# A decoder layer in float32 on one core: the opening staged by halves of columns, row maxima by quadrants, context products last, and indirect stores in a queue of their own

## What is computed

```python
def layernorm(x): return (x - mean(x)) / sqrt(var(x) + 1e-5)
# 1. self-attention, 16 heads of 16, ALiBi slopes 0.5**h
q, k, v = split(heads(layernorm(x) @ qkv_w.T + qkv_b))
scores = q @ k.T / 4 - abs(i - j) * slope[h]
x = x + (softmax(scores) @ v) @ out_w.T + out_b
# 2. cross-attention on 77 context rows, one head of 256
y = layernorm(x); a = softmax((y @ Wq.T + bq) @ (ctx @ Wk.T + bk).T / 16) @ (ctx @ Wv.T + bv)
x = x + (y + a) @ Wo.T + bo
# 3. mixture of 8 experts (256 -> 1024 -> 256), top 2 by the router
y = layernorm(x); w = softmax over the two largest of y @ W_router + b_router
x = x + sum over the two: w[e] * (relu(y @ W1[e] + b1[e]) @ W2[e] + b2[e])
```

## Time and profile before

| | |
|---|---|
| runs | 1726.36, 1726.41, 1731.1 us; median 1726.41 |
| the profiled execution | 1725.03 us, of which the span is 1723.2 |
| busy | PE 94%, DVE 59%, ACT 46%, POOL 19% of the span |
| mean granted PE clock | 0.976 of full |

### The profile page before, as it was taken

The page is one execution under the profiler, slowest core; times in us unless marked ns, Lnnn a source line. Parts: engine busy times, 40 slices in busy tenths (PEclk is TensorE's granted clock), DMA queues, the critical chain, the costliest instruction groups (busy, mean ns, idle before and its releaser), DMA issues.

```text
span 1723.2 us, 29797 instructions
## 1 busy us (share of the span) xinstructions
PE 1625.2 (94%) x10070; PEld 972.2 (56%) x10070; DVE 1024.4 (59%) x2366; ACT 787.4 (46%) x1635; POOL 321.7 (19%) x310
## 2 busy tenths in 40 slices
PE   3689999999999999999999999799999999999996
PEld 1333333344444434445434443259999899999986
DVE  3488878788778788777788676323354332333322
ACT  2107666667655666655665657562222122122211
POOL 5301120001210050310031100412134122221221
PEclk8779999999999999999999999899999999999999
DMA  6640413331313440314422603234566765656663
GB/s 178 150 85 25 78 17 62 41 41 32 71 26 78 65 91 1 41 38 90 78 55 38 133 10 119 100 124 134 139 190 185 203 175 169 197 171 179 175 166 74
DMA packets 90837, 173.31 MB, mean 101 GB/s; under 512 B 12947, under 2 KB 47763, under 8 KB 90560
## 3 DMA queue, kind: packets, MB, share of 16 engines
q1 hardware_dynamic: 74272, 143.69, 33.0%
q0 software_dynamic: 15744, 26.54, 7.3%
q10 hardware_dynamic: 672, 1.18, 0.3%
HBM read 133.69 MB, written 37.29 MB: 99 GB/s over the span
## 4 chain that ended last, share of the span: by engine, by line
PE 89%; DVE 3%; ACT 3%; DMA 2%; issue 2%; POOL 0%; SPq 0%; ACTq 0%; POOLq 0%; DVEq 0%
PE ps L1181 14%; PE ps L979 14%; PE ps L1163 14%; PE ps L1000 14%; PE ps L965 12%; PE ps L1030 3%; ACT prob L1193 2%; DVE rmax L1328 2%; PE ps L1039 2%; PE ps L1083 2%; PE ps L1052 2%; PE ps L1003 2%; PE ps L1021 2%; PE ps L968 2%; PE ps L1151 1%
## 5 line engine op out<-in xcount | busy, mean ns | idle before, releaser
L1328 DVE TENSOR_REDUCE rmax<-ps 128x1 f32<-128x512 f32 x1024 | 665.8, 686 | 234.9 <-PE ps L1003 125.3
L1193 ACT ACTIVATE prob<-ps 128x512 f32<-128x512 f32 x1024 | 562.4, 601 | 363.1 <-PE ps L968 185.8
L1000 PE MATMUL ps<-stacked_k,stacked_q 112*128 112x512 bf16 x1024 | 396.5, 391 | 22.9 <-DMA stacked_k<-parts_of_rows 15.0
L965 PE MATMUL ps<-stacked_q,stacked_k 115*128 115x512 bf16 x1024 | 361.8, 384 | 15.7 <-issue 8.0
L979 PE MATMUL ps<-prob,values 128*32 128x512 f32 x2048 | 276.3, 612 | 7.4 <-ACT prob L1193 7.2
L1000 PEld LDWEIGHTS ps<-stacked_k,stacked_q 112*128 112x128 bf16 x1024 | 99.8, 98 | 301.7 <-DVE rmax L1328 201.2
L1163 PEld LDWEIGHTS ps<-xiT,w_now 128*128 128x128 f32 x2272 | 265.2, 192 | 3.7
L1181 PE MATMUL ps<-w,hidT 128*128 x1136 | 260.0, 382 | 7.7 <-issue 6.0
L1163 PE MATMUL ps<-xiT,w_now 128*128 128x128 f32 x2272 | 266.9, 275 | 0.0
L1297 ACT ACTIVATE hidT<-ps,b 128x128 f32<-128x128 f32 x284 | 81.1, 368 | 356.3 <-PE ps L1163 318.6
L1181 PEld LDWEIGHTS ps<-w,hidT 128*128 128x128 f32 x1136 | 210.1, 190 | 40.3 <-issue 14.4
(11 more groups left out here) (181 smaller groups left out, 1146.6 us busy)
## 6 DMA issues: line engine op xcount, KB each, us to landing
w_now<-in_w SPq DMA_DIRECT2D x71, 1024.0 KB
stacked_q<-parts_of_rows SPq DMA_DIRECT2D x96, 128.0 KB, 5.7
stacked_k<-parts_of_rows SPq DMA_DIRECT2D x93, 128.0 KB, 6.6
xi<-expert_rows SPq DMA_DIRECT2D x71, 130.0 KB, 2.1
w<-in_w SPq DMA_DIRECT2D x8, 1024.0 KB, 9.5
parts_of_rows<-q_part SPq DMA_DIRECT2D x24, 256.0 KB, 3.6
parts_of_rows<-k_part SPq DMA_DIRECT2D x21, 256.0 KB, 4.9
xr<-in_x POOLq DMA_DIRECT2D x4, 1024.0 KB, 9.1
```

The lines of the kernel that those rows point to most:

```text
L965: m = e.matmul(ps[:, bank, :], ka[i][0:ROWS, hh, kt * P:(kt + 1) * P], qa[i][0:ROWS, hh, ch * BANK:(ch + 1) * BANK], start=True, stop=True)
L1000: m = e.matmul(ps[:, bank, :], qa[i][0:MAX_ROW, hh, qt * P:(qt + 1) * P], ka[i][0:MAX_ROW, hh, kc * BANK:(kc + 1) * BANK], start=True, sto ...
L1193: e.activation(prob[:, u % NPROB, :], ps[:, u % NSCORE, :], ACT.Exp).then_inc(sem["exp"], 1)
L1328: e.tensor_reduce(rmax[:, G % 2, hh * NT + qt, kc:kc + 1], ps[:, p.bank("max", *k), :], AX.X, ALU.max).then_inc(sem["maxed"], 1)
```

## The change

1. The first four projections go query 0, key 0, query 1, key 1. A new step `first_half` stages and spreads one half of the columns (512), for SP (all of the query rows, and the stage of key half 0) and ACT (the spreads of both key halves, and the stage of key half 1). The first half has a semaphore of its own, `first_rows`.
2. SP issues the position rows of sets 1 and 2 and the spread of group 1 only when `spread0` is complete.
3. The maxima of group 0 go by quadrants: 16 of (query half 0, key half 0), then (0, 1), (1, 0), (1, 1). The second quadrant waits for `spread0`.
4. The loop of the opening adds as many maxima as banks are free (two), then side work. The context products start only after 32 maxima.
5. The scatters of batches 0 to 2 are a queue of their own, `scattering`: at most one per score, each at least 0.7 after the planned end of the one before (planned at 1.3 each).

```diff
+def maxima_of(G):
+    if G:
+        return [(hh, qt, kc) for hh in range(HG) for qt in range(NT) for kc in range(NCH)]
+    halves = [(0, 0), (0, 1), (1, 0), (1, 1)]
+    return [(hh, NT // 2 * q + qt, kc) for q, kc in halves for hh in range(HG) for qt in range(NT // 2)]
@@ prepare(b)
-            for a in range(2):
-                for ch in range(NCH):
+            first = (b, mo) == (0, 0)
+            for one in range(2):
+                for other in range(2):
+                    a, ch = (other, one) if first else (one, other)
...
-            if b:
+            if first:
+                for ch in range(NCH):
+                    add("first_half", ch)
...
@@ route(b, tiles)
-        soon = b == NB - 2
-        blocks_known = table(0) if soon else iter(())
-        for tt in range(*tiles):
+        if whole:
+            scattering.append(scatters(b))
+            if b == NB - 2:
+                yield from table(0)
...
+    def scatters(b):
+        for tt in range(NT):
             for which in range(TOPK):
+                while p.pe < p.made.get("scatter", 0.0) + 0.7:
+                    yield
                 add("scatter", b, tt, which)
...
+                p.after["scatter", b, tt, which] = p.counts["exp"]
+                yield
@@ plan()
-    beside = [opening, context_products()]
+    beside = [opening]
+    context = [context_products()]
...
+        if context and now["maxima"] >= UNITS // 2:
+            beside.append(context.pop())
+        while bank_free() and now["maxima"] < UNITS + LEAD and now["spread"] > now["maxima"] // UNITS:
+            if next(maxima, "end") == "end":
+                maxima = all_maxima()
@@ sync
                     if G == 1:
                         e.wait_ge(sem["q_specials"], 16 * HG)
+                        e.wait_ge(sem["spread0"], spread_in(0))
...
+                elif kind == "first_half":
+                    ch, = k
+                    cols = slice(ch * BANK, (ch + 1) * BANK)
+                    for a in range(2 - ch):
+                        for n, part in enumerate(("high", "mid", "low")):
+                            e.wait_ge(sem[part], p.upto(part, 0, 0, a, ch))
+                            e.dma_start(stage[0, a, n, 0:P, cols], split[n][a][:, 0, cols]).then_inc(sem[("first_q", "first_k")[a]], 16)
+                    e.wait_ge(sem["first_q"], 16 * NPART * (ch + 1))
+                    for j, (of_q, _) in enumerate(PAIRS):
+                        e.dma_start(qa[0][DH * j:DH * (j + 1), :, cols], by_row(stage[0, 0, of_q, 0:HG * DH, cols])).then_inc(sem[("first_rows", "spread0")[ch]], 16)
```

More of the change, by code:

```diff
@@ L276, in prepare @@
                     yield 10
-            if b:
+            if first:
+                for ch in range(NCH):
+                    add("first_half", ch)
+                split.add((b, mo))
+                now["spread"] = 1
+                spread_when_ready()
+                yield 0
+            elif b:
                 staging.append(stage_out(b, mo))
@@ L396, in route @@
         yield 0
-        soon = b == NB - 2
-        blocks_known = table(0) if soon else iter(())
-        for tt in range(*tiles):
+        if whole:
+            scattering.append(scatters(b))
+            if b == NB - 2:
+                yield from table(0)
+        else:
+            for tt in range(*tiles):
+                for which in range(TOPK):
+                    add("scatter", b, tt, which)
+                    yield 0
+    def scatters(b):
+        for tt in range(NT):
             for which in range(TOPK):
+                while p.pe < p.made.get("scatter", 0.0) + 0.7:
+                    yield
                 add("scatter", b, tt, which)
-                if whole:
-                    p.after["scatter", b, tt, which] = p.counts["exp"]
-                next(blocks_known, None)
-                yield from pause(2 if whole and not soon else 1)
+                p.after["scatter", b, tt, which] = p.counts["exp"]
+                yield
     def table(which):
@@ L465, in row_maxima @@
     def row_maxima(G):
-        for hh in range(HG):
-            for qt in range(NT):
-                for kc in range(NCH):
-                    add("max", G, hh, qt, kc)
-                    add("maxed", G, hh, qt, kc)
-                    now["maxima"] += 1
-                    yield
+        for hh, qt, kc in maxima_of(G):
+            add("max", G, hh, qt, kc)
+            add("maxed", G, hh, qt, kc)
+            now["maxima"] += 1
+            yield
         add("nmax", G)
@@ L535, in plan @@
     now["late"] = True
-    beside = [opening, context_products()]
+    beside = [opening]
+    context = [context_products()]
     maxima = row_maxima(0)
     landed = float("inf")
-    while beside or p.pe < landed:
-        if bank_free() and now["maxima"] < UNITS + LEAD and next(maxima, "end") == "end":
-            maxima = all_maxima()
+    while beside or context or p.pe < landed:
+        if context and now["maxima"] >= UNITS // 2:
[3 more added lines that the diff above has]
+                maxima = all_maxima()
         flush()
@@ L594, in unit @@
             step_on(staging)
+            step_on(scattering)
         waiting = []
@@ L625, in plan @@
     flush()
+    while scattering:
+        step_on(scattering)
+        p.at["pe"] += 0.1
     while closing:
```

53 lines of the change are left out of this document (24 added, 29 removed).

## The result

| | before | after |
|---|---|---|
| median of 4 runs each, us | 1727.88 | 1712.12 |
| lowest and highest, us | 1726.36, 1731.1 | 1706.68, 1717.18 |
| ratio, 95% interval | | 0.9908 [0.9881, 0.9935] |
| profiled execution; its span, us | 1725.03; 1723.2 | 1717.18; 1715.3 |
| mean granted PE clock | 0.976 | 0.979 |

Faster by 15.8 us in the median; the forecast was 1713. The profiled execution of after is the slowest of its four runs, so the steps seen in it have to explain 7.9 us of span, and not 15.8. What may make up the rest is taken up under "The clock"; it is not shown.

What follows compares the result with a forecast made beforehand. PE was taken as the bound, busy 94% of the span, so only its stalls or half-clock stretches could give. Opening -11, batch 2's scatters -12 and the new wait +9.5 sum to -13.5: median 1713 us, 8 in 10 within 1703 to 1724.

Steps and rivals of the forecast that it cites:

- First half: first maximum at 37: Opening: with columns spread by halves, the first maximum starts at about 37 instead of 42.5.
- `spread0` at 44.5, third `rest` at 53, a wait of 6 us: Opening: `spread0` lands at 44.5, POOL's first `low` ends at 53, DVE then PE stand about 6 us before third `rest`.
- From the third `rest` to `nmax` 54.5: Opening: from 53, remaining side work, context steps and maxima bring `nmax` at 107.5 instead of 118.8.
- Opening -11: Opening of the kernel: `nmax` at 107.5 instead of 118.8, worth -11 us, bounds -5 and -17.
- rival B: Opening: POOL not in the way, `spread0` at 41 to 42, DVE waits 2 to 3 us; total 1704.5; chance 15%.
- Scatters of batch 2 -12: Last attention group: spreading batch 2's scatters removes ACT's stalls, -12 us, bounds 0 and -12.5.
- Rival A: Last attention group: spacing scatters does not free ACT; 1725, no change, or 1719 with half kept; chance 18%.
- The new wait +9.5: Start of experts: last two scatters end late, PE stands 7.5 us longer plus half clock, +9.5, bounds +7 and +12.
- Scatters of batches 0 and 1 at 0: Attention beside the scatters of batches 0 and 1: between -1 and +1 us, taken as 0.
- C: Last attention group: ACT is slowed as long as scatters run, making the kernel slower, 1733; chance 6%.
- D: Opening: context loads land after maximum 32, costing 5 us more, 1718; chance 5%.
- the same: Whole kernel: outcome of no measurable change in time, from most of A and the rest of D; chance 0.14.

Runs made afterwards that it cites:

- whole_columns: Changed kernel with the first 128 rows staged and spread by whole columns and the old order of projections (part 1 undone): 1712.14 us, ratio 0.9896 to before.
- opening_only: Changed kernel with the scatters of batches 0 to 2 put back as before, so parts 1 to 4 alone: 1711.18 us, ratio 0.9874 to before.
- dense_batch0: Changed kernel with the 16 scatters of batch 0 in one run, those of batches 1 and 2 still spread: 1726.89 us, ratio 0.9951 to before.
- weights_first: every3 with w1 of blocks 0 and 1 issued before the wait for the scatters: 1702.01 us, ratio 0.9837 to before.
- the change's stand-in: Changed kernel with SP issuing the position rows of sets 1 and 2 before waiting for `spread0`, on the third chip: 1714.1 us, ratio 0.9995 to before.
- every3: Changed kernel with batch 2's scatters one in every three scores, regardless of the planned end of the one before: 1707.76 us, ratio 0.9836 to before.

## Why the prediction was right, point by point

- **First half: first maximum at 37**, came at 33.6. 1.3 is the run's earlier start; the write took 1.8 and not 3, and the last spread landed 3.4 behind its issue and not 4.5. And the step was worth nothing by itself: 0.4 us in whole_columns. The prediction said that POOL's wait decides, but not that this empties the step.
- **`spread0` at 44.5, third `rest` at 53, a wait of 6 us**: 41.3, 49.85 and 6.32. Mechanism and size right, place 1.9 us early beside the earlier start: `spread0` is not 2 us later than before, as said, but at the same place.
- **From the third `rest` to `nmax` 54.5**: 51.75. Side work overlapped better than by my adding up.
- **Opening -11**: -17.2 in the profiled executions, -15.9 from the last key part on. The term was the worst of the three, at the edge of its bounds (-5 to -17), by the sizes above. This is rival B's number, and two of B's three reasons hold (`spread0` at 41 to 42, side work that overlaps well); its third, that POOL is hardly in the way, doesn't, for DVE waited 6.32 and not 2 to 3.
- **Scatters of batch 2 -12**: -12.4. Rival A falls wherever the stalls were seen (gone in after, back in opening_only, made in dense_batch0). One reading was off: the 25.1 us, with their 20 exponentials, run from the start of the four at 1101.64 and not from its end; the term isn't changed by it.
- **The new wait +9.5**: +10.8, and 2 for the half clock, together 12.8 against bounds of 7 to 12. The step that was mis-sized is "lands in 2 or more": `xi` of block 1 took 5.05, behind 2 MB of `w1`. weights_first took these out and it fell to T + 5.3.
- **Scatters of batches 0 and 1 at 0**: about right in sum, but of terms that cancel. Beside batch 0's scatters the new spacing gives 1.6 us (from `nmax` of group 8 to that of group 9, 60.2 in after; 61.8 in before and 62.3 in opening_only). From group 11 to group 12, ahead of batch 1's scatters, every trace with the queue takes 73.5, where before and opening_only take 71.5 and 71.4: 2 us that part 5 costs, and that the prediction didn't have.
- **Sum -13.5**: the three terms measured give -15.9 - 12.4 + 12.8 = -15.5, by the medians -15.8. The two mis-sized terms (-4.9 and +3.3) cancel for the most part, so the forecast of 1713 is nearer than its parts were, and that is luck. In the two profiled executions alone the span fell by 7.9.
- **C** (slower) and **D** (context late) fall: no ACT wait beside the spread scatters, `c_turn` at 73.28 without one.
- Not foreseen: that the gain belongs to the chip as much as to the kernel. On the third chip the change's stand-in is level with before, at a chance that I had given to "the same" for another reason.

## What to carry to other kernels

When a wait goes, ask at once which one it covered: here the context's wait covered POOL's, and moving nine load issues behind the parts that DVE waits for brought 6 to 8.6 us, where starting the maxima 8.2 us earlier had brought 0.4. Spreading transfers to spare an engine pays only if their end stays ahead of the one who waits for them; of that waiter's own transfers, those that need not wait (the weights) go first. And a change whose gain is a stall taken away should be timed on more than one chip.

## What the chip did that I had not expected

- A run of back-to-back indirect stores of 128 rows, one in 1.27 us, had PE, ACT and DVE stand at the same time, for up to 8.6 us, and cost 15.1 us for 16 of them in dense_batch0, with the DMA engines at 30% and POOL going on. At 1.3 to 2.1 us apart, 1.7 on average (every3), nothing stopped. On the chip of the last group ten of them in a row stopped nothing.
- PE's clock fell from 2.4 to 1.2 GHz for part of 8 to 16 us in stretches where PE was busy (12.00 of 12 us at 0.72), up to three times per execution, in one of two nearly equal programs and not in the other; that is 0 to 11.9 us of the span in the profiles above, as much as the spread between the runs of one kernel (10.5 us in the four of after).
- The kernel before takes 1714.05 us in one of the four groups of runs, and 1727.88 to 1732.15 in the others.
